# A constant folded from two weight matrices, built from row-group matmuls one unit a slot, with x and output rings of four

## What is computed

```python
def _L0_attn_ref(query, key_param, Wq, bq, Wk, bk, Wv, bv, Wo, bo):
    k = jnp.broadcast_to(key_param, (B, S, D_MODEL))
    queries = (query @ Wq + bq).reshape(B, L, H, E)
    keys_flat = k @ Wk + bk
    values = (keys_flat @ Wv + bv).reshape(B, S, H, D)
    keys = keys_flat.reshape(B, S, H, E)
    scores = jnp.einsum('blhe,bshe->bhls', queries, keys)
    A = sparsemax(scale * scores)
    out = jnp.einsum('bhls,bshd->blhd', A, values)
    out = jnp.transpose(out, (0, 2, 1, 3)).reshape(B, L, H * D)
    return out @ Wo + bo
...
x = _layernorm(x + attention(x))
s = x @ Win + bin_
g = sum over h of relu(s[..., None] * W1 + b1) * W2, + b2
x = _layernorm(x + g @ Wout + bout)
```

## Time and profile before

| | |
|---|---|
| median of 3 runs | 1581.36 us (1575.73 to 1583.24) |
| the profiled execution's own time | 1570.85 us |
| its span in the trace | 1569.1 us |
| PE, DVE, ACT, POOL busy | 90%, 70%, 70%, 42% |

### The profile page before, as it was taken

How to read it: one execution, slowest core, us unless ns; L and a number is a source line. 1 busy time by engine, 2 the same in 40 slices (tenths; PEclk the granted TensorE clock), 3 DMA queues, 4 the chain that set the end, 5 groups by cost and what they waited for, 6 DMA issues and landing times. The chain is left out here.

```text
span 1569.1 us, 25895 instructions
## 1 busy us (share of the span) xinstructions
PE 1415.4 (90%) x6102; PEld 915.1 (58%) x6102; DVE 1096.9 (70%) x4547; ACT 1105.0 (70%) x2402; POOL 655.8 (42%) x1645
## 2 busy tenths in 40 slices
PE   6887388799999999999999999999999999889984
PEld 5444144466666666666666666666666666545542
DVE  2654754578877877878788777888778777834454
ACT  3443143367787887788887787878888878867784
POOL 1221022223454444545544554444544444544444
PEclk9998698899999999999999999999999999989995
DMA  4333033655555555455545555555545555446753
GB/s 133 124 104 97 27 108 108 187 183 162 169 189 189 186 179 177 165 189 189 188 157 174 189 172 172 176 189 189 182 174 177 175 189 189 162 162 232 251 157 72
DMA packets 91798, 258.50 MB, mean 165 GB/s; under 512 B 15651, under 2 KB 15651, under 8 KB 75206
## 3 DMA queue, kind: packets, MB, share of 16 engines
q1 hardware_dynamic: 91590, 256.39, 49.0%
HBM read 206.00 MB, written 50.33 MB: 163 GB/s over the span
## 5 line engine op out<-in xcount | busy, mean ns | idle before, releaser
L610 PE MATMUL bank<-G_sb,pT 128*128 128x512 f32 x1024 | 465.7, 598 | 0.0
L977 DVE MAX8 top<-bank 128x8 f32<-128x32 f32 x2048 | 212.5, 181 | 146.9 <-issue 124.3
L610 PEld LDWEIGHTS bank<-G_sb,pT 128*128 128x128 f32 x1024 | 186.7, 192 | 186.9 <-issue 186.9
L419 POOL TENSOR_TENSOR shift_sq<-sum,per_row_sq 128x1 f32<-128x1 f32 x256 | 99.8, 390 | 413.1 <-DVE y_sb L883 412.8
L1019 DVE SCALAR_TENSOR_TENSOR acc<-hinge,w2c,acc 128x512 f32<-128x512 f32 x224 | 167.3, 747 | 61.3 <-ACT hinge L721 54.3
L721 ACT ACTIVATE hinge<-s_sb,b1c,w1c 128x512 f32<-128x512 f32 x256 | 205.7, 807 | 0.0
L706 ACT ACTIVATE unread<-y_sb,shift_sq 128x512 bf16<-128x512 f32 x256 | 183.1, 715 | 24.9 <-POOL minus_mean L421 24.8
L540 PE MATMUL bank<-A_hi,xT_hi 128*128 128x512 f32 x512 | 200.5, 392 | 0.0
L541 PE MATMUL bank<-A_lo,xT_hi 128*128 128x512 f32 x512 | 200.4, 391 | 0.0
L542 PE MATMUL bank<-A_hi,xT_lo 128*128 128x512 f32 x512 | 200.1, 391 | 0.0
L444 POOL TENSOR_TENSOR side<-side 128x256 bf16<-128x256 bf16 x128 | 86.6, 676 | 240.8 <-ACT side L793 240.8
(11 more groups left out here) (122 smaller groups left out, 2644.2 us busy)
## 6 DMA issues: line engine op xcount, KB each, us to landing
G_sb<-G_of_heads SPq DMA_DIRECT2D x128, 1024.0 KB, 5.4
x_sb<-in_L_attn_query_dram SPq DMA_DIRECT2D x128, 256.0 KB, 4.7
y_sb<-in_L_attn_query_dram SPq DMA_DIRECT2D x256, 128.0 KB, 5.4
out_dram<-o_sb SPq DMA_DIRECT2D x256, 128.0 KB, 4.7
G_of_heads<-y_sb SPq DMA_DIRECT2D x64, 256.0 KB, 2.6
y_sb<-in_L_attn_Wk_dram SPq DMA_DIRECT2D x1, 1024.0 KB, 5.6
y_sb<-in_L_attn_Wq_dram SPq DMA_DIRECT2D x1, 1024.0 KB, 8.2
y_sb<-in_L_attn_Wv_dram SPq DMA_DIRECT2D x1, 1024.0 KB
```

Source lines behind the costliest of these rows:

```text
L419: nc.gpsimd.tensor_tensor(shift_sq[:, par:par + 1], total[:, par:par + 1], per_row_sq[:], ALU.mult).then_inc(s_mean, 1)
L610: mm = nc.tensor.matmul(o_ps[i % 2][:], pT[:, bass.ds(pair_place(turn, i) + (i % H * C + c) * P, P)], G_sb[:, i % GR, c, :], start=(c == 0 ...
L977: mx = nc.vector.max(top8[:, h, :], z_ps[i % 2][:, h * S:(h + 1) * S])
```

## The change

Three things change.

1. **V is laid out differently.** `V_rep` holds each head's V four times side by side (one ACT copy of 128 x 2048), so that a matmul with the first 32 columns of the identity gives VT on all four groups of 32 partitions at once. 16 such matmuls with 32 columns fill one bank, and one copy of 128 x 512 brings it to `VT_rep`. The fills of `V_blk` and `first_place` on POOL are gone; `ones_row` has its own place.
2. **A piece is another part of G.** Piece k is (four heads, chunk c, row group a): a matmul over the 32 rows of partition group a of `VT_rep` and of `Wo`, into bank a of four. The four pieces of a unit (a = 0 to 3) belong to one slot, so the 64 pieces stand in slots 1 to 16. `bo` is added by one matmul where c and a are both 0, so 4 times. Each store is still 128 rows of 2 KB, now to four heads.
3. **The rings of x and of the output tile have 4 places in place of 2.**

```diff
-        XR, YR, OR, UR, HR = 2, 16, 2, 8, 2
+        XR, YR, OR, UR, HR = 4, 16, 4, 8, 2
...
-            k = 3 * (turn * UNROLL + j - 1) if isinstance(turn, int) else PIECES
-            return range(max(k, 0), max(min(k + 3, PIECES), 0))
+            unit = turn * UNROLL + j - 1
+            return range(HPC * unit, HPC * unit + HPC) if 0 <= unit < PIECES // HPC else range(0)
+
+        def piece(k):
+
+            return k // (HPC * C), k // HPC % C, k % HPC
...
-                    sp.dma_start(G_dram[h, :, c * D:(c + 1) * D], y_sb[:, k % STAGES, :]).then_inc(
-                        s_Gst[k % STAGES], 16)
+                    sp.dma_start(G_dram[HPC * heads:HPC * heads + HPC, a * S:(a + 1) * S, c * D:(c + 1) * D],
+                                 y_sb[:, k % STAGES, :]).then_inc(s_Gst[k % STAGES], 16)
...
-            nc.gpsimd.memset(V_blk[:], 0.0).then_inc(s_const, 1)
...
-                    for n in range(C):
-                        for a in range(H // C):
-                            mm = nc.tensor.transpose(G_ps[n][:, a * P:(a + 1) * P], V_blk[:, n * (H // C) + a, :],
-                                                     ident[:])
-                        mm.then_inc(s_vT, 1)
+                    for h in range(H):
+                        mm = nc.tensor.matmul(G_ps[0][:, h * S:(h + 1) * S],
+                                              V_rep[:, h * P:(h + 1) * P],
+                                              ident[:, 0:S], start=True, stop=True)
+                    mm.then_inc(s_vT, 1)
...
-                    if c == 0:
-                        nc.tensor.matmul(G_ps[k % C][:], first_place[:], bo_row[:], start=True, stop=False)
-                    nc.tensor.matmul(G_ps[k % C][:], VT_blk[:, h, :], Wo_sb[:, c, :], start=(c > 0),
-                                     stop=True).then_inc(s_Gmm, 1)
+                    with_bo = c == 0 and a == 0
+                    if with_bo:
+                        nc.tensor.matmul(G_ps[a][:], ones_row, bo_row[:], start=True, stop=False)
+                    nc.tensor.matmul(G_ps[a][:], VT_rep[rows, heads * P:(heads + 1) * P], Wo_sb[rows, c, :],
+                                     start=not with_bo, stop=True).then_inc(s_Gmm, 1)
...
-                    for a in range(HPC):
-                        rows = slice(a * S, (a + 1) * S)
-                        cp = nc.scalar.copy(V_blk[rows, :, rows], ps[rows, :].rearrange("p (h d) -> p h d", h=H))
-                    cp.then_inc(s_sev, 1)
+                    nc.scalar.copy(V_rep.rearrange("p (h a d) -> p h a d", h=H, a=HPC),
+                                   ps[:].rearrange("p (h d) -> p h d", h=H).unsqueeze(2).broadcast_to(
+                                       [P, H, HPC, E])).then_inc(s_sev, 1)
```

More of the change, by code:

```diff
@@ L151, in build_kernel @@
         G_sb = sb("G_sb", [P, GR, C, D])
-        V_blk, VT_blk = (G_sb[:, r].rearrange("p c n -> p (c n)").rearrange("p (h n) -> p h n", h=H)
-                         for r in range(2))
+        V_rep, VT_rep = G_sb[:, 0].rearrange("p c n -> p (c n)"), G_sb[:, 1, 0, :]
         G_dram = nc.dram_tensor("G_of_heads", [H, P, C * D], F32, kind="Internal").ap()
@@ L158, in build_kernel @@
         bo_row = sb("bo_row", [1, D])
-        first_place = sb("first_place", [1, P])
+        ones_row = sb("ones_row", [1, P])[:]
         Win_sb = sb("Win_sb", [P, C, M])
@@ L191, in build_kernel @@
         bq_c = sb("bq_c", [P, C])
-        ones_row = above[0:1, 0:P]
         kpT4, keysT4 = (r.rearrange("p (c n) -> p c n", c=C) for r in (o_sb[:, 0, :], o_sb[:, 1, :]))
@@ L297, in build_kernel @@
         KEY_LOADS, Q_LOADS, WLOADS = 3, 2, 16
-        FILLS = 15 + S
-        CONSTS = FILLS + 5
+        FILLS = 13 + S
+        CONSTS = FILLS + 4
         @block.sync
@@ L342, in slot @@
                 for k in pieces(turn, j):
-                    h, c = k // C, k % C
+                    heads, c, a = piece(k)
                     sp.wait_ge(s_Gev, k + 1)
-                    sp.dma_start(G_dram[h, :, c * D:(c + 1) * D], y_sb[:, k % STAGES, :]).then_inc(
-                        s_Gst[k % STAGES], 16)
+                    sp.dma_start(G_dram[HPC * heads:HPC * heads + HPC, a * S:(a + 1) * S, c * D:(c + 1) * D],
+                                 y_sb[:, k % STAGES, :]).then_inc(s_Gst[k % STAGES], 16)
                 if in_range(turn, j, LAG_G):
@@ L350, in slot @@
                     if isinstance(turn, int) and base + i < H:
-                        if h < GR:
+                        if h == 0:
                             sp.wait_ge(s_Gmm, PIECES)
-                        for k in range(C * h, C * h + C):
-                            sp.wait_ge(s_Gst[k % STAGES], 16 * (k // STAGES + 1))
+                        if h % HPC == 0:
+                            for r in range(STAGES):
+                                sp.wait_ge(s_Gst[r], 16 * (h // HPC + 1) * (HPC * C // STAGES))
                     if not isinstance(turn, int) or base + i >= GR:
@@ L403, in _ @@
             nc.gpsimd.memset(go_on[:, :, 0:1], 0.0).then_inc(s_const, 1)
-            nc.gpsimd.memset(first_place[:, 0:S], 1.0).then_inc(s_const, 1)
             for n, row in enumerate((0, E)):
-                pool.wait_ge(s_const, FILLS + 2 + n)
+                pool.wait_ge(s_const, FILLS + 1 + n)
                 nc.gpsimd.memset(pick_c[row:row + 1, :].bitcast(F32), 1.0).then_inc(s_const, 1)
-            pool.wait_ge(s_const, FILLS + 4)
+            pool.wait_ge(s_const, FILLS + 3)
             nc.gpsimd.affine_select(out=ident[:], in_=ident[:], compare_op=ALU.not_equal, fill=1.0,
@@ L635, in slot @@
                     nc.tensor.matmul(f_ps[:], acc_lo[:, here], Wout_hi[:], start=False, stop=True).then_inc(s_f, 1)
-                if isinstance(turn, int) and base + j == 0:
-                    for n in range(C):
-                        for a in range(H // C):
-                            mm = nc.tensor.transpose(G_ps[n][:, a * P:(a + 1) * P], V_blk[:, n * (H // C) + a, :],
-                                                     ident[:])
-                        mm.then_inc(s_vT, 1)
-                for k in pieces(turn, j):
-                    h, c = k // C, k % C
-                    if c == 0:
[L646 to L651, removed]
-                        nc.tensor.matmul(G_ps[k % C][:], first_place[:], bo_row[:], start=True, stop=False)
-                    nc.tensor.matmul(G_ps[k % C][:], VT_blk[:, h, :], Wo_sb[:, c, :], start=(c > 0),
-                                     stop=True).then_inc(s_Gmm, 1)
+                if turn == 0 and j == 0:
+                    for h in range(H):
[3 more added lines that the diff above has]
+                    mm.then_inc(s_vT, 1)
+                for k in pieces(turn, j):
+                    heads, c, a = piece(k)
+                    rows = slice(a * E, (a + 1) * E)
+                    pe.wait_ge(s_vTc, 1)
+                    if k >= HPC:
+                        pe.wait_ge(s_Gev, k - HPC + 1)
+                    with_bo = c == 0 and a == 0
[3 more added lines that the diff above has]
+                                     start=not with_bo, stop=True).then_inc(s_Gmm, 1)
             slots(pe, slot)
@@ L804, in slot @@
                 probabilities(turn, j, 1)
[L805 to L810, removed]
+                if turn == 0 and j == 0:
+                    act.wait_ge(s_vT, 1)
+                    nc.scalar.copy(VT_rep, G_ps[0][:]).then_inc(s_vTc, 1)
                 for k in pieces(turn, j):
@@ L814, in slot @@
                         act.wait_ge(s_Gst[k % STAGES], 16 * (k // STAGES))
-                    nc.scalar.copy(y_sb[:, k % STAGES, :], G_ps[k % C][:]).then_inc(s_Gev, 1)
+                    nc.scalar.copy(y_sb[:, k % STAGES, :], G_ps[k % HPC][:]).then_inc(s_Gev, 1)
             slots(act, slot)
```

1 line of the change is left out of this document (removed).

## The result

The changed kernel takes 1643.15 us (median of 4 runs, 1642.35 to 1644.52), the kernel before 1582.3 us (1575.73 to 1586.68): a ratio of 1.0389 (1.0351 to 1.0427), 3.9% slower. The forecast was 1531 us and the range ended at 1562. The profiled execution has a span of 1641.0 us against 1569.1.

A forecast was written before the change was run, and what follows sets the result against it. It took the filling to be bound by a ring through SP and the full slots by PE. Terms 0.7 - 3 - 24 - 18 - 6 = -50.3 us on 1570.85 gave 1520.5, with 10.5 added 1531 us; range 1502 to 1562.

The forecast's parts named there:

- the stores of a slot: Slots 1 to 16: the fourth store lengthens SP's part by nothing beyond its copy; x lands 3.31 us after issue.
- The third rival: Slots 1 to 16: PE stays at 1.2 GHz while G is built, +80 us, 1611 us; chance 0.07.
- Slots 1 to 16 apart from the store: Filling with four pieces a slot: 8.1 to 8.5 us against 8.66; -3 us taken, ends -10 and +10.
- Slots 17 to 22: Filling without pieces: loads of x run ahead and DVE is late next; -24 us taken.
- The full slots: Output ring of four ends ACT's wait for the store, so PE waits less; -18 us, ends 0 and -30.
- The emptying: DVE's 53.3 us of waits for stores go, 5.5 us of it showing in PE; -6 us, ends 0 and -16.
- V laid out anew: At the start: one copy for four, 16 two-pass matmuls for 16 transpositions; +0.7 us, range -1 to +3.
- The first rival: Full slots and emptying stay as they are because the stores were hidden anyway; 1555 us, chance 0.18.
- The second: Filling: the pieces do not overlap, eight passes a slot, 8.5 us and more; 1546 us, chance 0.15.
- The sum: Whole kernel: -50.3 us on an execution of 1570.85 gives 1520.5; 10.5 us added for the median, 1531.

The follow-up runs named there:

- e1_s_outer: The changed kernel with VT_rep's columns ordered pattern first, head second, so the store's outermost dimension is 32 in place of 4: 1496.64 us, 0.946 of the kernel before.

## Why the prediction was wrong

**The step that failed** is the one on the stores of a slot: "The fourth store of a slot waits for the last copy as the third did, so it lengthens SP's part by nothing beyond its copy." I costed the store as an issue of SP, took it over with its 128 rows of 2 KB, and kept 3.31 us for the landing of x behind it. That the shape was now 4x32x512 stood in SP's list, and I read it as the same transfer. It moved the load's landing to 11.4 us, and this with the clock that fell in the wait made slots 1 to 16 longer by 145.5 us, where I had -3, with +10 as the end. Slot 3 shows the shares: 18.2 us in the changed kernel, and 8.5 in the matching slot of e1_s_outer. Of the 9.7 us between them 8.4 are the landing (11.4 against 3.0), 0.85 lie between x and the last copy, where PE ran at the lower clock at first, and 0.5 between the last copy and the issue of the load. The slow store was not among the rivals. The third rival was near in its place and its time (slots 1 to 16, 1611 us) and wrong in its cause: the turned store, with the same short pieces, took the slot back to 8.75 us, at a mean clock of 0.86 where it had been 0.68. The short pieces by themselves cost no more than that. Its argument that no more than two slots in a row stay cold was weak already before: slots 21 to 23, three in a row, were granted 0.69, 0.76 and 0.82 on average.

The other steps, one by one.

- *Slots 1 to 16 apart from the store.* Forecast -3 for the 16 slots, in e1 180.3 - 183.1 = -2.8. That they agree is partly luck: slots 1 to 8 were 0.6 us longer together and not shorter, and the gain came from the later ones. The single slot was 8.75 and not 8.1: a store of three dimensions costs SP 0.60 us of issue against 0.32, so the load of x goes out 1.1 us after the last copy and not 0.4. That the copies end last was a reckoning in the prediction and not yet seen in a trace; in e1 the pieces end at 62.72 and the copies at 65.35.
- *Slots 17 to 22.* Forecast -24; -28.7. The slots without a check took 5.1 to 7.1 us, and the wait of 6.65 us is gone.
- *The full slots.* Forecast -18; -35.4. The mechanism was right, the size was not: I took 18 of the 24 us of listed waits, and the listed waits were not all. A window of the full slots before, and in the changed kernel (columns as in the earlier trace rows):

```profile
600.00:800.00 200.00, 192.85 (x872) 128.61 (x871) 156.33 (x644) 161.65 (x351) 95.87 (x236) 1.00 0.51 176
```

```profile
600.00:800.00 200.00, 200.00 (x916) 135.24 (x915) 164.02 (x687) 170.82 (x371) 101.72 (x247) 1.00 0.54 185
```

  PE was idle for 7.15 of 200 us before, which is 32 us in 87 slots, most of the 35.4; in the changed kernel it is never idle there, so 9.90 us a slot is PE's own work.
- *The emptying.* Forecast -6; -12.6, within the stated end. Why it is twice as much is not shown.
- *V laid out anew.* Forecast +0.7 with +3 as the end; +5.3. The upper end that the text itself worked out, 32 passes of 0.19 us, 6.1 us, was the right one for the matmuls (6.28 us in place of 3.03): a pass with 32 moving columns took 0.196 us, as long as a transposition with 128. I took too little of it. The other 2 us are the clock: the scores of slot 0, behind this step, take 5.3 us at a granted clock of 0.55 in place of 3.05 us at 1.00. One of their matmuls before, and in the changed kernel:

```profile
35.43 0.40 PE L540 MATMUL bank<-A_hi,xT_hi 128*128 128x512 f32 x1
```

```profile
38.71 0.63 PE L540 MATMUL bank<-A_hi,xT_hi 128*128 128x512 f32 x1
```

- *The first rival*, that the output ring is hidden, falls by the two runs of the rings. *The second*, that the pieces do not overlap, falls by 1.14 us for eight passes.
- *The sum.* Without the store the span would have been 75.2 us shorter (e1: 1493.9 against 1569.1), half as much again as the forecast's 50. The 10.5 us between the median and the profiled execution of before, which I added back to the prediction, were not the kernel's constant: in no kernel with the output ring of 4 is the median more than 1 us above the profiled execution. That these 10 us were waits for stores is likely, and not shown by itself.

## What to carry to other kernels

When a change alters the access pattern of a DMA, read its outermost dimension before its bytes. Here 4 left the store on four engines' worth of bandwidth, where 32 and 128 did not. The cost fell on the next transfer in line and not on the one that was changed, and turning the order of rows at the source (in one copy of 128 x 512) mended it for nothing: slot 1 begins at 44.2 us with it and at 44.1 without. Price an issue list by what each transfer holds up behind it. And a ring of buffers helps where the wait is for a place (the output tile); where the load waits for its turn in an in-order list, move the load ahead instead.

## What the runs showed of the hardware

- Four row groups of a float32 matmul with 32 rows and 512 columns, two passes each, take 1.14 us together at the full clock, against 3.70 us for four full ones.
- A store with an outermost dimension of 4 kept the DMA engines busy to 0.26 and moved 100 to 105 GB/s, and four of them in a row delayed a load with 128 rows outermost by 8.1 us (11.4 against 3.3). SP's own time to issue that load rose from 0.46 to 2.58 us.
- SP takes 0.32 us to issue a store of 128x512 and 0.60 us for 32x4x512 of the same bytes.
- The load of x waited for held PE for 11 us a slot, and the granted clock was 0.50 before PE came back (94 to 96 us above); the transposition of x then took 1.11 us in place of 0.66.
